# Attention scores of a small language-model tower in two matmul passes instead of three

## The reference

```
h = layernorm(concat(emb[x], window3_mean(pca[x]) @ proj_w + proj_b) @ fus_w + fus_b)
h = h + attention_block(layernorm(h))   # 16 heads of 64, softmax, its own residual and layernorm
h = h + ffn_block(layernorm(h))         # 16 experts, top 2, capacity per expert, its own layernorm
```

```
scores = (x Wq + bq) (x Wk + bk)^T / 8
attn   = softmax(scores, over keys)
y      = x + (attn (x Wv + bv)) Wo + bo
out    = (y - mean) / sqrt(var + 1e-3) * gamma + beta
```

## Time and profile before

| | |
|---|---|
| median of 3 runs | 537.13 us (536.72 to 547.7) |
| the profiled execution | 537.01 us, span 535.2 us |
| busy over the span | PE 93%, DVE 84%, POOL 72%, ACT 71% |
| mean granted clock of PE | 0.989 |

### The profile page before, as it was taken

The page is one execution under the profiler, slowest core; times in us unless marked ns, Lnnn a source line. Parts: engine busy times, 40 slices in busy tenths (PEclk is TensorE's granted clock), DMA queues, the critical chain, the costliest instruction groups (busy, mean ns, idle before and its releaser), DMA issues. The chain is left out here.

```text
span 535.2 us, 15239 instructions
## 1 busy us (share of the span) xinstructions
PE 497.3 (93%) x5567; PEld 362.8 (68%) x5567; DVE 447.9 (84%) x1054; ACT 379.2 (71%) x768; POOL 384.7 (72%) x519
## 2 busy tenths in 40 slices
PE   5988799999999999999999998769999999999984
PEld 3876567777777777776777775534466767777664
DVE  4797669999999999998999999868778898878675
ACT  2868778888898888988898887336766555556530
POOL 1025669888788888888888888750468798789783
PEclk9998989999999999999999999999999999999998
DMA  6800000000000000000000000000734163351011
GB/s 233 333 6 2 2 2 4 2 3 3 3 2 3 3 3 3 4 2 4 3 4 2 3 3 2 2 1 4 168 80 100 23 150 76 77 138 38 31 40 60
DMA packets 11902, 21.68 MB, mean 41 GB/s; under 512 B 4668, under 2 KB 9780, under 8 KB 10164
## 3 DMA queue, kind: packets, MB, share of 16 engines
q1 hardware_dynamic: 11410, 20.15, 13.8%
q10 hardware_dynamic: 418, 0.55, 0.4%
HBM read 16.24 MB, written 4.33 MB: 38 GB/s over the span
## 5 line engine op out<-in xcount | busy, mean ns | idle before, releaser
L845 POOL TENSOR_TENSOR s_pl<-s_pf,s_ph 128x512 f16<-128x512 f32 x128 | 147.0, 1160 | 8.7 <-ACT s_ph L959 8.7
L1062 DVE TENSOR_REDUCE s_mx<-ps 128x4 f32<-128x512 f32 x128 | 83.8, 677 | 17.6 <-PE ps L1225 14.1
L953 ACT ACTIVATE s_pf<-ps,s_ln_r 128x512 f32<-128x512 f32 x128 | 87.1, 683 | 11.4 <-PE ps L1238 8.9
L823 PE MATMUL ps<-s_xt_all,s_w1s 128*128 128x512 f16 x384 | 87.9, 379 | 2.2 <-ACT s_ub L1543 1.6
L1698 PE MATMUL ps<-s_w2s,s_hid 128*128 128x256 f16 x768 | 88.9, 273 | 0.0
L1698 PEld LDWEIGHTS ps<-s_w2s,s_hid 128*128 128x128 f16 x768 | 75.1, 98 | 11.0
L959 ACT ACTIVATE s_ph<-s_pf 128x512 f16<-128x512 f32 x128 | 74.0, 637 | 0.0
L1273 PE MATMUL ps<-s_zh,s_cth 128*128 128x256 f16 x256 | 69.9, 273 | 1.0 <-DVE s_ctl L1096 1.0
L1273 PE MATMUL ps<-s_zl,s_cth 128*128 128x256 f16 x256 | 69.8, 273 | 0.0
L1273 PE MATMUL ps<-s_zh,s_ctl 128*128 128x256 f16 x256 | 69.8, 273 | 0.0
L823 PEld LDWEIGHTS ps<-s_xt_all,s_w1s 128*128 128x128 f16 x384 | 37.3, 98 | 41.4 <-ACT s_ub L1543 2.1
(11 more groups left out here) (246 smaller groups left out, 1149.0 us busy)
## 6 DMA issues: line engine op xcount, KB each, us to landing
s_rep<-picks SPq DMA_DIRECT2D x14, 512.0 KB, 6.7
s_stage<-in_w SPq DMA_DIRECT2D x2, 1024.0 KB, 14.3
out<-s_zh SPq DMA_DIRECT2D x16, 128.0 KB, 2.0
out<-s_lg SPq DMA_DIRECT2D x16, 128.0 KB, 1.7
s_stage<-in_wq SPq DMA_DIRECT2D x1, 1024.0 KB, 5.0
...
```

Of the source, the lines that this page charges most:

```text
L823: mm = nc.tensor.matmul(hidden_bank(n)[:], w1s[:, wp, c, j * P:(j + 1) * P], xt_all[:, GB * g:GB * (g + 1), xp, c, :], start=(k == 0), sto ...
L845: nc.gpsimd.tensor_tensor(flat(pl[:, b % 2, 4 * j:4 * j + 4, :]), pf[:, j, :], flat(ph[:, b % 2, 4 * j:4 * j + 4, :]), ALU.subtract).then_ ...
L953: nc.scalar.activation(pf[:, j, :], ST[j % 2][:], ACT.Exp, bias=ln_r[:, b:b + 1]).then_inc(exp_done[j], 1)
L1062: nc.vector.tensor_reduce(mx[:, b % 2, c:c + 4], A[ab][:].rearrange("p (h k) -> p h k", h=4), AX.X, ALU.max).then_inc(max_done[hf][ab], 1)
```

## The change

The key operand of `score_cols` is no longer the counts times `r12`, split in two parts, but the counts themselves as `nkT`, one float16 tile, so the pass with the rest goes. The factor `r12` of the key is given to the exponential as its scale (ACT, an operand tile beside the bias). The columns `ONE` and `SHIFT` of the token rows become pairs: on the key side they hold the high and the low float16 part of the factor `s12`, `R2` those of `s1`. `nkT` is made in the first stage: PE turns `nb` a second time (`nkt_part`, in place of the first two runs of dummy matmuls and before the first table), ACT evicts four of the eight results and DVE four (`nkt_cols`). ACT's copy of the counts to `nk` goes to a later place. The factor rows of `nkT` can't be turned there; at the start of the second stage `scale_rows` turns them on PE, DVE copies them to `srow`, and SP copies them by 12 DMAs into `nkT`. `SHIFT` having two rows, SP copies each `mrow` twice for each half: four DMAs for a sequence instead of two. DVE does `log_rho` before its third-round token rows, which move by a slot.

The core of the diff:

```diff
@@ -41,4 +41,4 @@
 UD = 64
-R2, ONE, SHIFT = 2 * V, 2 * V + 1, 2 * V + 2
-ONE_HI, UV = R2 + 2, R2 + 4
+R2, ONE, SHIFT = 2 * V, 2 * V + 2, 2 * V + 4
+UV = ONE + 2
 RHO_SCALE = 0.25
@@ -121,3 +121,4 @@
         uh, ul = sb("uh", [P, 2, B, UD], F16), sb("ul", [P, 2, B, UD], F16)
-        u_top, u_rest, nk = uh[:, 0], ul[:, 0], uh[:, 1]
+        u_top, nk = uh[:, 0], uh[:, 1]
+        nkT = ul[:].rearrange("p a b u -> p (a b u)").rearrange("p (b t) -> p b t", t=P)
         r12, ln_r = sb("r12", [P, B]), sb("ln_r", [P, B])
...
@@ -200,2 +201,3 @@
         UT_BANKS = [psum[n] for n in (2, 3, 6, 7)]
+        NKT_BANKS = [psum[n] for n in (1, 2, 3, 5, 2, 3, 1, 5)]
         TABLE_BANKS = [psum[4], psum[5], psum[4]]
@@ -264,4 +266,4 @@
                 pool.wait_ge(cleared, CLEARED["uf_0"])
-                nc.gpsimd.memset(uf[:, :, ONE:SHIFT + 1], 1.0).then_inc(cleared, 1)
-                pool.wait_ge(nt_ready, 4)
+                nc.gpsimd.memset(uf[:, :, ONE:ONE + 1], 1.0).then_inc(cleared, 1)
+                pool.wait_ge(nt_ready, 12)
                 nc.gpsimd.memset(nb[:, :, R2:R2 + 1], 1.0).then_inc(cleared, 1)
...
@@ -302,4 +304,6 @@
                         .then_inc(nt_ok, 1)
-                act.wait_ge(n_ok, 2)
-                nc.scalar.activation(nk[:, :, 0:2 * V], nb[:, :, 0:2 * V], ACT.Copy)
+                for n in range(4):
+                    act.wait_ge(nt_ready, 4 + n + 1)
+                    nc.scalar.activation(nkT[:, 4 * n:4 * n + 4, :].rearrange("p b t -> p (b t)"), NKT_BANKS[n][:], ACT.Copy)\
+                        .then_inc(nt_ok, 1)
                 act.wait_ge(cs_ready, 1)
@@ -325,4 +329,4 @@
                     nc.scalar.activation(qkv_t[:, n], TABLE_BANKS[n][:].rearrange("p (c u) -> p c u", c=HD), ACT.Copy).then_inc(qkv_ok, 1)
-                    act.wait_ge(qkv_ok, 2 * n + 1)
-                    if n < 2:
+                    act.wait_ge(qkv_ok, (1, 3, 6)[n])
+                    if n == 0:
                         nc.scalar.activation(qkv_t[:, n, :, ONE:ONE + 1], bT[:, n, :].rearrange("p (c o) -> p c o", o=1), ACT.Copy)\
...
@@ -343,2 +347,3 @@
                     nc.scalar.activation(wo_v[:, c, :], wo_v[:, c, :], ACT.Identity, bias=wsum[:, 1, c:c + 1]).then_inc(wo_step, 1)
+                nc.scalar.activation(nk[:, :, 0:2 * V], nb[:, :, 0:2 * V], ACT.Copy)
                 root_1()
@@ -444,2 +449,10 @@
                                       twice(psum[7][:, 0:2 * KC * UD].rearrange("p (x u) -> p x u", u=UD))).then_inc(mt_ok, 1)
+
+                def nkt_cols(n):
+                    dve.wait_ge(nt_ready, 8 + n + 1)
+                    nc.vector.tensor_copy(nkT[:, 16 + 4 * n:20 + 4 * n, :].rearrange("p b t -> p (b t)"), NKT_BANKS[4 + n][:])\
+                        .then_inc(nkt_ok, 1)
+
+                nkt_cols(0)
+                nkt_cols(1)
                 dve.wait_ge(cs_ok, 1)
...
@@ -582,3 +597,15 @@
-                keep_going(15, psum[0][:, 0:FREE])
+                def nkt_part(n):
+                    if 1 <= n < 4:
+                        pe.wait_ge(nt_ok, (1, 2, 4)[n - 1])
+                    elif n >= 4:
+                        pe.wait_ge(nt_ok, 4 + (2, 3, 1, 4)[n - 4])
+                    for k in range(4):
+                        for ab in range(2):
+                            mm = nc.tensor.matmul(NKT_BANKS[n][ab * UD:(ab + 1) * UD, k * P:(k + 1) * P], nb[:, 4 * n + k, :], ident16[:],
+                                                  start=True, stop=True)
+                    mm.then_inc(nt_ready, 1)
+
+                for n in range(4):
+                    nkt_part(n)
                 pe.wait_ge(in_id, 16)
@@ -591,3 +618,4 @@
-                keep_going(6, psum[0][:, 0:FREE])
+                nkt_part(4)
+                nkt_part(5)
                 pe.wait_ge(mt_ok, 1)
...
@@ -674,3 +702,6 @@
+                nkt_part(6)
+                nkt_part(7)
                 table(0, range(3))
+                pe.wait_ge(nkt_ok, 2)
                 quads(0)
...
@@ -831,2 +865,7 @@
                 sp.dma_start(countdown[:], d["countdown"]).then_inc(in_cd, 16)
+                sp.wait_ge(srow_step, 2)
+                for ab in range(2):
+                    for r, j in ((R2, 0), (R2 + 1, 1), (ONE, 2), (ONE + 1, 3), (SHIFT, 2), (SHIFT + 1, 3)):
+                        r += ab * UD
+                        sp.dma_start(nkT[r:r + 1, :, :], srow[:, j, :]).then_inc(in_srow, 16)
                 for b in range(B):
@@ -834,5 +873,5 @@
                     for ab in range(2):
-                        r = ab * UD + SHIFT
-                        sp.dma_start(qh[r:r + 1, b % 2].rearrange("o f t q -> o (f t) q"),
-                                     mrow[8 * ab:8 * ab + 8, b % 2, :]).then_inc(shift_in[b % 2], 16)
+                        for r in range(ab * UD + SHIFT, ab * UD + SHIFT + 2):
+                            sp.dma_start(qh[r:r + 1, b % 2].rearrange("o f t q -> o (f t) q"),
+                                         mrow[8 * ab:8 * ab + 8, b % 2, :]).then_inc(shift_in[b % 2], 16)
@@ -952,3 +991,3 @@
                         act.wait_ge(ln_ok, 4)
-                    nc.scalar.activation(pf[:, j, :], ST[j % 2][:], ACT.Exp, bias=ln_r[:, b:b + 1]).then_inc(exp_done[j], 1)
+                    nc.scalar.activation(pf[:, j, :], ST[j % 2][:], ACT.Exp, bias=ln_r[:, b:b + 1], scale=r12[:, b:b + 1]).then_inc(exp_done[j], 1)
@@ -970,3 +1009,3 @@
                     if b >= 2:
-                        act.wait_ge(shift_in[b % 2], 32 * (b // 2))
+                        act.wait_ge(shift_in[b % 2], 64 * (b // 2))
                     nc.scalar.activation(mrow[:, b % 2, :], MISC[0:H, 0:P], ACT.Copy, scale=-1.0).then_inc(mrow_done, 1)
...
@@ -1131,4 +1170,6 @@
-                DVE_TOKENS = {(-5, 0): (2,), (-5, 1): (5,), (-5, 2): (8,), (-4, 0): (11,), (-4, 1): (13, 14)}
+                DVE_TOKENS = {(-5, 0): (2,), (-5, 1): (5,), (-5, 2): (8,), (-4, 1): (11,), (-4, 2): (13, 14)}
+                dve.wait_ge(srow_step, 1)
+                nc.vector.tensor_copy(srow[:].rearrange("b j t -> b (j t)"), MISC[0:B, :]).then_inc(srow_step, 1)
                 nc.vector.memset(cn[:].rearrange("p h t (a u) -> p (h t a) u", u=UD)[:, :, UV:UD], 0.0).then_inc(cn_zero, 1)
@@ -1137,8 +1178,9 @@
                         q_lo(i + 5, 1)
-                    for n in DVE_TOKENS.get((i, 0), ()):
-                        token_rows(n)
-                    if has(i + 2):
-                        context_lo(i + 2, 1)
                     if i == -4:
                         log_rho()
+                    elif i < -4:
+                        for n in DVE_TOKENS.get((i, 0), ()):
+                            token_rows(n)
+                    if has(i + 2):
+                        context_lo(i + 2, 1)
                     if has(i + 3):
@@ -1230,3 +1272,5 @@
                     if hf == 0:
-                        pe.wait_ge(shift_in[b % 2], 32 * (b // 2) + 32)
+                        pe.wait_ge(shift_in[b % 2], 64 * (b // 2) + 64)
+                        if b == 0:
+                            pe.wait_ge(in_srow, 16 * 12)
                     for n in range(2):
@@ -1234,7 +1278,7 @@
                             pe.wait_ge(exp_done[2 - 2 * hf + n], b + hf)
-                    for n, (part, q) in enumerate(((0, qh), (0, ql), (1, qh))):
+                    for n, q in enumerate((qh, ql)):
                         for ab in range(2):
                             r = slice(ab * UD, ab * UD + UD)
-                            mm = nc.tensor.matmul(ST[ab][:], ub[r, b, part, :], flat(q[r, b % 2, hf]),
-                                                  start=(n == 0), stop=(n == 2))
+                            mm = nc.tensor.matmul(ST[ab][:], nkT[r, b, :], flat(q[r, b % 2, hf]),
+                                                  start=(n == 0), stop=(n == 1))
                     mm.then_inc(st_ready[hf], 1)
@@ -1301,3 +1345,11 @@
+                def scale_rows():
+                    for j in range(4):
+                        mm = nc.tensor.matmul(MISC[0:B, j * P:(j + 1) * P], nk[:, :, R2 + j:R2 + j + 1].rearrange("p b o -> p (b o)"),
+                                              identh[:], start=True, stop=True)
+                    mm.then_inc(srow_step, 1)
+
                 def maxima_cols(b):
+                    if b == 0:
+                        pe.wait_ge(srow_step, 2)
                     for n in range(2):
@@ -1326,2 +1378,3 @@
+                scale_rows()
                 for i in STEPS:
```

More of the change, by code:

```diff
@@ L186, in build @@
         R1_STEP, T3_STEP, R2_STEP = 5, 8, 12
-        nk_step = sem("nk_step")
+        nk_step, nkt_ok = sem("nk_step"), sem("nkt_ok")
         uf_ok, uh_ok, ul_ok, ut_ready, ut_ok, ut_last = (sem(n) for n in ("uf_ok", "uh_ok", "ul_ok", "ut_ready", "ut_ok", "ut_last"))
@@ L279, in _ @@
                 pool.wait_ge(nk_step, 3)
-                for n, src in ((R2, s1), (ONE_HI, s12)):
+                for n, src in ((R2, s1), (ONE, s12)):
```

(22 more changed lines are left out.)

4 lines of the change are left out of this document (2 added, 2 removed).

## The result

The changed kernel took 560.60 us (median of 4, 558.84 to 561.36), the kernel before, on the same chip, 539.67 us (median of 4, 536.72 to 547.70). The ratio is 1.040, with a 95% interval of 1.032 to 1.048: slower. The profiled execution took 558.84 us with a span of 557.0, against a span of 535.2 before: 21.8 us more.

The account below looks back on a forecast made before the run. PE looked full, but the shift's DMA loop was to bind at 9.2 us a round. 537.0 + 1.2 (first stage) - 1.5 (lead-in) + 20.3 (rounds) - 0.2 (last pass) = 556.8, 557 us; range 543 to 573, 8 in 10.

Parts of the forecast that it names:

- The pass less: In `score_cols`: one pass is worth 0.215 us, two go in a round, so 0.43 us of PE.
- Two DMAs more: SP's four issues per `mrow` close a loop through PE's wait ahead of `score_cols`: round 9.2 us, 20.3 us more over 29.
- over 1 us: Expected sign: PE idle ahead of `score_cols(b, 0)` for the DMA of `s_mrow`, over 1 us each in nearly every round.
- The 50 ns for a dispatch: The skill's figure for the sequencer's dispatch: by it the two more issues would cost 0.1 us and the forecast be wrong.
- The 0.09 us ahead of `x_cols`: PE's time between third pass and `x_cols`, put down to the loop through POOL and taken off PE's part of the round.
- The 1.85 to landing: Time taken from the last shift DMA's issue to landed, chosen near the upper bound of 1.93; lower bound 1.32 us.
- The scale operand: ACT's exponentials: 0 to 0.11 us more for each of four, at most 0.45 us a round, nothing in time.
- First stage: DVE's last two evictions ahead of its product cost 1.2 us; 2.5 if the first two are late, or nothing.
- The rival on the clock: PE's idle time in the rounds lowers its clock: 583 us if in every second round; 5 in 100.
- Lead-in: Before the rounds: `ln_r` ahead of token rows takes back 1.5 us; with SP's 12 issues, between -2.3 and +5.
- POOL's loop at 8.38: Rival: issues don't stand in the way, the loop from y's squares through POOL and PE binds; 533 us; 8 in 100.
- The 7.98: Rival: the whole pass is gained, PE alone sets a round of 7.98 us; 521 us, 3% faster; 3 in 100.

## Why the prediction was right

Forecast 557 us, measured 560.6, in the profiled execution 558.84; slower, as forecast with 84 in 100. The mechanism was the one forecast; that the sum came within 2 us of the profiled execution is in part luck, since errors of both signs cancel in it. By its steps:

- *The pass less.* A pitch of 174.39 - 174.16 = 0.23 us, as 0.215 forecast. It left PE, and the time hardly moved: the run with two issues has the pass gone and is within 0.4% of the kernel before. That PE is full everywhere was not the bound; the loop beside it was.
- *Two DMAs more.* The term that decides. Forecast 4.78 + 0.59 + 0.02 + 1.965 + 1.85 = 9.2, measured 4.88 + 0.59 + 0.02 + 2.01 + 1.74 = 9.24: +0.10, +0.05 and -0.11, which cancel. The wait for `s_mrow` came in 31 rounds, but with 0.7 us each, not "over 1 us": PE also sits idle 0.2 us ahead of `values` now, in 20 of the 22 rounds between 100 and 300 us, and the profile names nothing that ended it. 30 rounds gave 20.1 us, 29 were forecast with 20.3. The runs with 2, 3 and 4 issues, and with 4 in the kernel before, show it to be the cause. The 50 ns for a dispatch that the prediction took from the Trainium skill (DMA: Bandwidth & Descriptors, on the anatomy of one DMA) stand there for DMAs that GpSimd issues. The ones here are SP's, so the figure was never a rival for them: each more costs the loop 0.63 us where the loop binds.
- *Its terms.* The 0.10 is a misreading. The 0.09 us ahead of `x_cols` was put down to POOL and taken off; in the changed kernel nothing waits for `s_xc` between 100 and 300 us, and the gap is 174.70 - 174.39 = 0.31 as before. PE alone would need 8.07 us a round by that, not 7.98. The 0.05 is one too: two issues that take 1.31 us with 635 ns for the last start 0.675 apart, not half of 1.31; the earlier trace rows gives no distance. The 1.85 to landing was a choice between 1.32 and 1.93.
- *The scale operand.* Forecast 0 to 0.11 us each and nothing in time: 0.09 us, and nothing.
- *First stage.* The mis-sized term. Forecast 1.2 with 2.5 as upper end, measured 2.7 in the profiled execution. At the full clock it is 1.3, and 0.7 with the dummies in it; that PE's clock would fall there, with the dummy matmuls gone and PE idle 0.56 and 0.31 us between turned counts, I had called "beside that". The rival on the clock looked at the rounds, and it fell in the first stage.
- *Lead-in.* Forecast -1.5, measured -2.0, from 22.6 to 20.6 us. Two things cancel in part in it. At the full clock the same code takes 18.6 to 18.7 us, 4.0 less than the kernel before, which had falls of its own (0.83 between 40 and 50 and between 60 and 70 us). But in the profiled execution the clock fell between 48 and 54 us. The prediction had no term for either. "No wait for `ln_r`" was wrong: 1.17 us of 2.33 stayed. The 12 issues took 0.591 us each, 7.57 us in all, and ended at 57.9 in the changed kernel, when the first `mrow` started at 58.9: out of the way by 1 us. Where the clock did not fall, they ended as that `mrow` did, within 0.04 us.
- *The rivals.* POOL's loop at 8.38 was real: it is the round of the three kernels with two issues and the old order on PE and ACT, at 8.47 to 8.50, and why the change gains only 0.1 us a round even with the issues mended. The 7.98 was never reached. PE's clock held in the rounds of the changed kernel; in two other profiles with four issues it fell once and twice, behind late transfers.
- *The range.* Its low end does not follow from its terms: 537.0 + 1.2 - 1.5 - 0.2 + 5 is 541.5, not 543.
